# The second half of one feed-forward layer placed between the chunks of the next, normalisations on ScalarE, look-up bits on VectorE

## The reference, cut to what matters

```python
x = x + _L0_xattn_ref(_layernorm(x), ctx_1024, ...)   # 16 heads of 128
x = x + _L0_ffn_ref(_layernorm(x), ...)               # input, weights and hidden in blocks of 32, quantised
x = x + _L1_xattn_ref(_layernorm(x), ctx_1024, ...)   # weights depend on the context alone, applied to norm(x)
x = x + _L1_ffn_ref(_layernorm(x), ...)               # silu(gate) * up, hidden 1024
x = x + _L2_xattn_ref(_layernorm(x), ctx_1024, ...)   # 16 heads of 16, two key groups, q and k normalised
x = x + _L2_ffn_ref(_layernorm(x), ...)               # weights are lut[index], 16 values, hidden 688
x = x + _L3_xattn_ref(ctx_1024, _layernorm(x), ...)   # a state space scan over the context, 16 states
x = x + _L3_ffn_ref(_layernorm(x), ...)               # Hadamard transforms, hidden 1024
```

## Time and profile before

| what | value |
|---|---|
| median of 3 runs (lowest, highest) | 1029.34 us (1029.27, 1031.43) |
| the profiled execution, its span | 1028.96 us, 1027.4 us |
| mean granted TensorE clock, as a share of 2.4 GHz | 0.922 |
| busy: TensorE, VectorE, ScalarE, GpSimd | 867.6, 708.8, 535.8, 448.0 us |
| the chain that ended last, by engine | TensorE 30%, VectorE 14%, ScalarE 4%, GpSimd 1% |

### The profile page before, as it was taken

The page is one execution under the profiler, slowest core; times in us unless marked ns, Lnnn a source line. Parts: engine busy times, 40 slices in busy tenths (PEclk is TensorE's granted clock), DMA queues, the critical chain, the costliest instruction groups (busy, mean ns, idle before and its releaser), DMA issues.

```text
span 1027.4 us, 13071 instructions
## 1 busy us (share of the span) xinstructions
PE 867.6 (84%) x4348; PEld 615.1 (60%) x4352; DVE 708.8 (69%) x1367; ACT 535.8 (52%) x991; POOL 448.0 (44%) x274
## 2 busy tenths in 40 slices
PE   5795899999999999645579986858688799999998
PEld 3354777777877777513354643728577685545646
DVE  4247689999899998778848566765989863353311
ACT  2486687787778778733313442535678472112120
POOL 1211678777778886556810002007458540600000
PEclk8898899999999999866879998958699899999999
DMA  4003000100000100000520000000000001100000
GB/s 126 16 5 133 16 17 16 31 15 15 15 15 15 31 3 6 1 0 1 198 83 0 1 1 1 1 0 1 2 1 2 1 1 48 83 0 1 12 9 21
DMA packets 12924, 24.25 MB, mean 24 GB/s; under 512 B 4280, under 2 KB 8656, under 8 KB 11728
## 3 DMA queue, kind: packets, MB, share of 16 engines
q1 hardware_dynamic: 12448, 20.53, 6.2%
q10 hardware_dynamic: 432, 3.15, 0.8%
HBM read 22.63 MB, written 1.05 MB: 23 GB/s over the span
## 4 chain that ended last, share of the span: by engine, by line
PE 30%; DVE 14%; issue 4%; ACT 4%; POOL 1%; ACTq 0%; DVEq 0%
PE PS L2131 12%; PE PS L2180 6%; PE PS L2234 3%; DVE mxf L1574 2%; DVE regD L1612 1%; PE PS L2035 1%; PE PS L1674 1%; DVE regB L1612 1%; PE PS L2011 1%; PE PS L2198 1%; PE PS L2049 1%; PE PS L2218 1%; PE PS L2219 1%; DVE xn L1051 1%; PE PS L2083 1%
## 5 line engine op out<-in xcount | busy, mean ns | idle before, releaser
L487 POOL TENSOR_TENSOR X<-X,xn 128x512 f32<-128x512 f32 x62 | 103.4, 1668 | 69.1 <-ACT xn L712 68.6
L454 POOL TENSOR_SCALAR veps<-mv 128x4 f32<-128x4 f32 x16 | 3.6, 228 | 265.9 <-DVE mv L1042 265.8
L1141 DVE TENSOR_TENSOR_SCAN regB<-regB 128x1024 f32<-128x1024 f32 x32 | 85.5, 2671 | 0.2
L1122 DVE TENSOR_SCALAR_CACHE_REDUCE regA<-PS,nrq 128x256 bf16<-128x256 f32 x128 | 56.0, 475 | 38.2 <-PE PS L1749 36.3
L731 ACT ACTIVATE regA<-PS,nb,rq 128x256 f32<-128x256 f32 x128 | 72.1, 576 | 11.7 <-DVE regA L1122 10.9
L2234 PE MATMUL PS<-regA 128*128 128x128 f32 x512 | 74.8, 293 | 3.4 <-ACT regA L994 3.3
L480 POOL TENSOR_TENSOR y<-y,regB 128x1024 f32<-128x1024 f32 x32 | 75.7, 2364 | 3.5 <-DVE regB L1152 3.4
L1771 PE MATMUL PS<-regA 128*128 128x256 f32 x256 | 67.0, 384 | 7.3 <-DVE qss L1109 7.2
L2234 PEld LDWEIGHTS PS<-regA 128*128 128x128 f32 x512 | 68.2, 206 | 7.1 <-ACT regA L994 6.1
L1749 PE MATMUL PS<-regA 128*128 128x256 f32 x256 | 67.1, 385 | 0.0
L1780 PE MATMUL PS<-regA 128*128 128x256 f32 x256 | 66.5, 383 | 0.0
(11 more groups left out here) (276 smaller groups left out, 2162.6 us busy)
## 6 DMA issues: line engine op xcount, KB each, us to landing
regA<-in_W SPq DMA_DIRECT2D x16, 384.0 KB, 3.0
regB<-in_wg SPq DMA_DIRECT2D x2, 1024.0 KB, 6.5
regB<-in_wu SPq DMA_DIRECT2D x2, 1024.0 KB, 8.5
X<-in_x SPq DMA_DIRECT2D x1, 1024.0 KB, 8.2
regC<-in_wg ACTq DMA_DIRECT2D x1, 1024.0 KB, 5.8
regC<-in_wu ACTq DMA_DIRECT2D x1, 1024.0 KB, 8.0
regC<-in_wd ACTq DMA_DIRECT2D x1, 1024.0 KB, 10.0
regB<-in_wd SPq DMA_DIRECT2D x1, 1024.0 KB, 9.9
```

Of the source, the lines that this page charges most:

```text
L487: pool.tensor_tensor(xt, xt, part, ALU.add).then_inc(x0_add, 1)
L1122: ins = dve.tensor_scalar(spill[:, i, q, :], bank(S_BANK + i)[:, q * S:(q + 1) * S], nrq[par][:, t:t + 1], None, ALU.mult, ALU.min, accum_ ...
L1141: dve.tensor_tensor_scan(v(hs), v(dA), v(dBu), 0.0, ALU.mult, ALU.add).then_inc(scan_done, 1)
```

## The change

1. *Order.* Layer 0's feed-forward stops after four tiles for the first half's norm, the first half of attention 1 and the second half's; tile 4 and 5's gate and up follow, and tiles 6 and 7, all the second half's transposes and down products, and attention 1's second half are placed between the chunks of layer 1's feed-forward, first half. Attention 1 goes by batches of two tiles. Layer 2's keys begin after chunk 5 of the first half, and its first half's down products and norms lie between them.
2. *Norms 2 to 8.* ScalarE applies them (`ln_apply`), one activation for each tile with rstd as scale and -mean times rstd as bias; GpSimd's `ln_pow` makes that product with two more operations. TensorE transposes by tile. Norms 0, 1 and 9 to 15 stay on VectorE.
3. *Scan.* The last state's decay goes into a buffer of its own (over `u3`), so that ScalarE needn't wait for the state before. Its scans stand behind tile 3; one broadcast of the state before uses another PSUM bank. SP waits for the last scan, not for the last sum, before it loads layer 1's weights.
4. *Look-up.* VectorE makes the three masks and bit 0 by bitwise ands on the integers; ScalarE reads bit 0 as an integer. GpSimd's conversion, comparisons and subtractions go.

```diff
+        ACT_LN = range(2, 9)
 def ln_pow(n):                                          # GpSimd
     pool.wait_ge(ln_mv, n + 1)
-    link(pool.tensor_scalar(veps[:, :], mv[:, :, 1], LN_EPS, None, ALU.add))
-    pool.tensor_tensor(rstd[:, :], veps[:, :], neghalf[:, 0:TPH], ALU.pow).then_inc(ln_rstd, 1)
+    if n >= 3:
+        pool.wait_ge(*xn_ready(n - 1))
+    ready = pool.tensor_scalar(veps[:, :], mv[:, :, 1], LN_EPS, None, ALU.add)
+    if n in ACT_LN:
+        ready = pool.tensor_scalar(nmean[:, :], mv[:, :, 0], -1.0, None, ALU.mult)
+    link(ready)
+    power = pool.tensor_tensor(rstd[:, :], veps[:, :], neghalf[:, 0:TPH], ALU.pow)
+    if n in ACT_LN:
+        link(power)
+        pool.tensor_tensor(nmr[:, :], nmean[:, :], rstd[:, :], ALU.mult).then_inc(ln_rstd, 1)
...
+def ln_apply(n):                                        # ScalarE
+    act.wait_ge(ln_rstd, n + 1)
+    act.wait_ge(*xn_read(n - 1))
+    for t in range(TPH):
+        act.activation(xn[:, t, :], X[:, t0 + t, :], ACT.Identity, scale=rstd[:, t:t + 1],
+                       bias=nmr[:, t:t + 1]).then_inc(xn_tile, 1)
...
-            sp.wait_ge(wt_out, 6)
-            sp.wait_ge(y_done, 2 * NST + 1)
+            sp.wait_ge(scan_done, 2 * NST + 1)
             for tile, name in ((wf_g, "wg1"), (wf_u, "wu1"), (wf_d, "wd1")):
                 sp.dma_start(tile, a[name]).then_inc(ld_f1, 16)
+            sp.wait_ge(wt_out, 6)
...
 # VectorE, layer 0's feed-forward, after the new order
+            x_scales(0)
+            x_units(0)
+            round_values(rows(xv), rows(x8))
+            layer_norm_stats(3)
             state_scan(NST - 2, 1)
...
+            ffn0_gated(3)
+            ffn0_round(2)
+            ffn0_add(0)
+            layer_norm_tiles(4, (0,))
+            state_in(NST - 1, 0)
...
+            layer_norm_mean(4)
+            state_scan(NST - 1, 0)
+            state_scan(NST - 1, 1)
+            attend1_add(0)
+            layer_norm_tiles(5, (0, 1))
+            attend1_add(1)
...
+            state_out(NST - 1, 0)
+            ffn0_gated(4)
+            state_out(NST - 1, 1)
+            ffn0_round(4)
+            ffn0_gated(5)
+            gate(0, 0, 0)
+            ffn0_round(5)
+            gate(0, 0, 1)
+            ffn0_gated(6)
...
+            ffn0_add(7)
+            layer_norm_stats(6)
+            dve.wait_ge(y_done, 2 * NST + 1)
+            keys_step(0)
+            gate(0, 0, 6)
+            keys_step(1)
+            gate(0, 0, 7)
+            keys_step(2)
+            ffn_add(0, 0, 0)
+            attend1_add(2)
+            attend1_add(3)
+            layer_norm_stats(7)
...
 # TensorE, layer 1's feed-forward, first half
+            for c in range(FC):
+                if c < 2:
+                    pe.wait_ge(h0_done, 11 + c)
...
+                gate_up(0, 0, c, wf_g, wf_u, half[0])
+                if c == 1:
+                    ffn0_gate_up(6)
+                    hidden_transpose(4)
+                elif c == 2:
+                    ffn0_down(4)
+                    hidden_transpose(5)
+                    ffn0_gate_up(7)
+                elif c in (3, 4):
+                    ffn0_down(c + 2)
+                    hidden_transpose(c + 3)
+                elif c == 5:
+                    ffn0_down(7)
+                    pe.wait_ge(ld_2, 16 * 13)
+                    keys_values(0)
+            pe.wait_ge(kv2_out, 3)
+            ln_transpose(6)
+            down(0, 0, 0, wf_d)
...
+            attend1(2)
+            pe.wait_ge(df_add, 1)
+            attend1(3)
+            pe.wait_ge(x1_add, 3)
+            down(0, 0, 1, wf_d)
+            keys_values(1)
...
 def lut_step(i, step):                                  # VectorE
     A = w2[:, i * LP:(i + 1) * LP]
+    if step == 0:
+        for m, bit in zip(lut_m[i % 2], (2, 4, 8)):
+            dve.tensor_scalar(m.bitcast(I32), A.bitcast(I32), bit, None, ALU.bitwise_and).then_inc(lut_mask, 1)
+        dve.tensor_scalar(lut_b0[i % 2].bitcast(I32), A.bitcast(I32), 1, None, ALU.bitwise_and).then_inc(lut_bits, 1)
```

More of the change, by code:

```diff
@@ L196, in build @@
         invx, scx = [inv8[1], sb("mx_ix", [P, BLK])], [sc8[2], sb("mx_sx", [P, BLK])]
-        QX = [0, 2]
-        QH = [1] + [tt + 2 for tt in range(1, NT)]
+        QX = [0, 5]
+        QH = [1, 2, 3, 4, 6, 7, 8, 9]
         wq1, wk1 = tA(P), tA(P)
@@ L719, in decay @@
                     act.wait_ge(scan_done, 1)
+                elif isinstance(n, int) and n == NST - 1:
+                    act.wait_ge(zero_set, 1)
+                    act.activation(dA_last[:, c, :, 1:], dt3[:, c, :, 1:], ACT.Exp,
+                                   scale=A3[:, c, n:n + 1]).then_inc(dA_done, 1)
+                    return
                 else:
@@ L2106, in scan_transpose, with gate_up, down, ffn @@
                     last.then_inc(z_tr, 1)
-            def ffn(f, wg, wu, wd, nch):
-                hid = INTER2 if f == 1 else FF
+            def gate_up(f, hf, c, wg, wu, src):
+                i = CB[2 * f + hf] + c
+                rows = min(P, (INTER2 if f == 1 else FF) - c * P)
+                for w, to in ((wg, 2 + i % 2), (wu, 4 + i % 2)):
+                    for k in range(KD):
+                        last = pe.matmul(bank(to)[0:rows, :], w[:, k, c * P:c * P + rows], src[:, k, :],
+                                         start=k == 0, stop=k == KD - 1)
+                last.then_inc(guf_mm, 1)
+            def down(f, hf, t, wd):
+                td = TPH * (2 * f + hf) + t
+                nch = FCH[f]
+                for c in range(nch):
+                    rows = min(P, (INTER2 if f == 1 else FF) - c * P)
+                    if t == 0:
+                        pe.wait_ge(gated, CB[2 * f + hf] + c + 1)
+                    last = pe.matmul(bank(6 + td % 2)[:, 0:DIM], hT[0:rows, c, t * P:(t + 1) * P], wd[0:rows, c, :],
+                                     start=c == 0, stop=c == nch - 1)
+                last.then_inc(df_mm, 1)
+            def ffn(f, wg, wu, wd):
                 for hf in range(2):
@@ L2175, in ffn @@
                             ln_transpose(13)
-                        for c in range(nch):
-                            rows = min(P, hid - c * P)
-                            if t == 0:
-                                pe.wait_ge(gated, CB[m] + c + 1)
-                            last = pe.matmul(bank(6 + td % 2)[:, 0:DIM], hT[0:rows, c, t * P:(t + 1) * P], wd[0:rows, c, :],
-                                             start=c == 0, stop=c == nch - 1)
-                        last.then_inc(df_mm, 1)
@@ L2183, in ffn @@
-                        if f == 0 and hf and 1 <= t <= 2:
-                            pe.wait_ge(q2_out, 1)
-                            keys_step(4 * B + t)
-            ln_transpose(5)
-            pe.wait_ge(ld_f1, 48)
-            pe.wait_ge(ld_2, 16 * 13)
-            ffn(0, wf_g, wf_u, wf_d, FC)
+                        down(f, hf, t, wd)
+            half = [xnT[:, :, hf * HALF:(hf + 1) * HALF] for hf in range(2)]
+            pe.wait_ge(ld_f1, 48)
+            pe.wait_ge(ssm_use, 4 * NST + 1)
@@ new lines, in _ @@
+            ln_transpose(7)
+            pe.wait_ge(df_add, 2)
+            down(0, 0, 3, wf_d)
+            pe.wait_ge(xnT_done, TRANSPOSED.index(7) + 1)
+            keys_step(6)
+            for c in range(FC):
+                if c in (1, 5):
+                    if c == 1:
+                        pe.wait_ge(df_add, TPH)
+                    keys_values((7 + c) // 4)
+                pe.wait_ge(gated, FC + c - 1)
+                gate_up(0, 1, c, wf_g, wf_u, half[1])
+                keys_step(7 + c)
+                if c == 4:
+                    pe.wait_ge(stk_out, 8)
+                    ln_transpose(8)
@@ L2191, in scores @@
+            pe.wait_ge(stk_out, 12)
+            queries(0)
+            pe.wait_ge(kv2_out, 12)
+            for t in range(TPH):
+                pe.wait_ge(df_add, TPH + t - 1)
+                down(0, 1, t, wf_d)
+                if 1 <= t <= 2:
+                    pe.wait_ge(q2_out, 1)
+                    keys_step(4 * B + t)
             def scores(b, h):
```

565 lines of the change are left out of this document (319 added, 246 removed).

## The result

The changed kernel takes 1021.62 us (median of 4 runs, 1021.07 to 1023.47) against 1029.39 (1029.27 to 1031.43, 4 runs) beside it; the ratio is 0.9915, interval 0.9903 to 0.9926. The forecast was 1003, 989 to 1018: the direction is right, but where 26 us were forecast, 7.8 came.

A forecast was written before the change was run, and what follows sets the result against it. A serial VectorE stage (quantising, with GpSimd) before a serial TensorE stage was taken to bound the kernel; 25.7 us from reordering plus 0.4 from look-up bits, 26 off 1028.96, gave 1003 us, range 989 to 1018.

The forecast's parts named there:

- first chunk: Start of the second layer's feed-forward on TensorE: forecast at 499 in place of 529.7, a gain of 30.7 us.
- merged stretch: From the first chunk to the end of that layer's last down product: 141 us against 136.0, bounds 126 and 151.
- look-up stage: From that last down product to the next layer's first chunk, third attention included: 185.9 us, 0.4 gained.
- Start of the tiles: First layer's feed-forward: normalisation on ScalarE and an earlier first block maximum start the first tile's matmuls near 437, 3.8 us earlier.
- Tiles 0 to 3: First layer's feed-forward: VectorE pays some 4.3 us per tile; fourth gating at 461, its addition at 471, scans 472 to 477.
- First half of attention 1 moved up: Second attention's first half before the first chunk: GpSimd's power ends at 478, banks free at 496, 3 us allowed for collisions.
- rival C: More is gained: TensorE's clock stays at 2.4 GHz, no collisions, bits hide; 4 + 4 + 5 us more, 990; chance 0.12.
- Look-up bits: Third attention: bits on VectorE cost 13.8 us, conditional copies lose 12.0; net 0.4 gained, bounds 12 gained and 14 lost.
- rival D: Slower: VectorE's bits open gaps before TensorE in the third attention and its clock falls; 1039; chance 0.05.
- A: Rival: the merged stretch becomes bound by VectorE, 151 us in place of 141; 1013; chance 0.18 together with E.
- E: Rival: normalisation on ScalarE gives nothing, as its queue stands at it; 3.8 and 4 us go, 1011; 0.18 with A.
- B: Rival: the look-up bits cost all they add, 14 us lost rather than 0.4 gained; 1017; chance 0.10.

The follow-up runs named there:

- experiment 6: Changed kernel with one added wait: VectorE starts the last two scans only once GpSimd has made the fourth layer norm's factors; 1013.54 us, ratio 0.983.
- experiment 7: Changed kernel with 18 extra, unused TensorE matmuls in its 4.5 us of idle time before the fourth layer norm's transposes; 1018.71 us, ratio 0.9887.
- experiment 9: Changed kernel with experiment 6's wait, shift weights made by ScalarE, and ScalarE's eighth layer norm copies put ahead of its key casts; 998.07 us, ratio 0.9691.
- experiment 5: Changed kernel with layer norms 2 to 8 applied by VectorE again, new order and look-up bits kept; 1020.22 us, ratio 0.9891.
- experiment 3: Changed kernel with experiment 6's wait and the look-up bits back on GpSimd; 1014.94 us, ratio 0.984.

## Why the prediction was wrong, step by step

The span came out 18.2 us above the forecast's 1001.4. The first chunk was 10.8 us late (509.8, not 499), the merged stretch 13.4 too long (154.4, not 141), and the look-up stage 6.0 shorter than forecast. Two steps failed: the path from tile 0 to the first chunk, above all the first half of attention 1, where I priced GpSimd's wait for the scans but not the idle TensorE and the low clock behind it; and the length of the second half's chunks in the merged stretch, 55.8 us where I had 46.9. That the direction was right is in large part luck: of the 19.9 us won, 18.4 were given back, and 6.4 of the 7.8 us of gain come from a stage for which I had 0.4.

*What bounds the kernel.* Right in kind: moving the feed-forward up shortened the serial VectorE stage, and what is won ahead of the first chunk arrives at the end (7.0 for 6.8 us in experiment 6, 3.0 for 3.2 in experiment 7). *Start of the tiles:* 439.1, not 437. GpSimd made the factors when it had before (from 426.3), so the 2.1 us arose in the block. About 1 of them is my arithmetic: 0.6 added and 0.55 and 0.6 saved make 433.5 for the end of the quantising, not 432.5. Besides, ScalarE's four activations took 2.07 us and not 1.8, and one 128x32 scaling took 1.13 in place of 0.18, beside a GpSimd addition.

*Tiles 0 to 3.* The fourth gating started at 463.1 (forecast: 461), as late as the first tile had been. From there the additions slipped: the fourth one started at 477.8, not 471. My cost per tile left out that the second half's quantising itself collides (its product takes 2.93 us, where the first half's took 1.23; two roundings take 2.89 us, one alone 0.69), and that the additions wait for TensorE, which waits for GpSimd's products. This is one part of the failed path to the first chunk: at the fourth layer norm's mean 7.1 us are lost (479.1, not 472).

*First half of attention 1 moved up.* Here the other half fails. That GpSimd waits out the scans was in the forecast and happened, 484.9 being 1.4 us behind the scans' end; the Trainium skill's rule that the port pair is held for a whole instruction (SBUF — State Buffer, Who interferes with whom) agrees with 2.11 against 0.23 us. What I didn't see is the consequence: the wait puts TensorE to idle and then to the low level, and with one engine's result feeding the next, every lengthened matmul is on the chain. From the fourth layer norm's mean to the fifth's I gave 16 us (472 to 488); it took 20.1 (479.1 to 499.2), and 10.6 more to the first chunk, for which I gave 8 and 3 of allowance. Experiments 6 and 7 show it: the two groups of attention matmuls alone take 3.5 us less at the full level, and with the one wait added, mean to mean takes 12.5 us. I had counted the low level as a gain of rival C if it went away, never as a cost of the new order. Of 10.8 us of lateness at the first chunk, one wait that lets GpSimd go first takes 6.8 off.

*Weights.* Right: they were issued behind the scans, and no wait for them is seen in any version.

*The merged stretch*, 141 with 151 as its upper bound, was 154.4. Its pieces by my own milestones, counted from the first chunk (496 in the forecast, 509.8 here):

| | forecast | measured |
|---|---|---|
| end of chunk 5 | 30 | 33.2 |
| end of chunk 7 | 41 | 43.6 |
| last down product of the first half | 68.6 | 73.5 |
| last chunk of the second half | 115.5 | 129.3 |
| last down product | 139.6 | 154.4 |

The largest miss, 8.9 us, is in the second half's chunks, for which I allowed 46.9 us. The kernel before takes 51.8 for the same chunks (from 593.2 to 645.0), so 5 us of the miss are a step that I should have checked against the trace. The other 4 are what the wait for ScalarE's copies grew by (4.16 us, 1.76 before) and the low level behind it (the keys' products take 4.51 us, 2.81 before); in experiment 9 the same moves win 4.7 us back. TensorE was busy 130.4 us where I had 126: 10.5 of moved work and not 9, on 118.5 where I had cut out 117, and some 1.4 left over, which I put down to the lower clock. My bound of 151 (its terms, 136.0, 3.6 and 12.5, make 152) assumed that only VectorE's queue can lengthen the stretch; ScalarE's order did too. "The shift weights still collide" was right, with the same 8.2 us; that a wait of this size costs 2.4 more behind it I had not seen (the kernel before pays 1.8 of that too, so it lengthened the stretch little).

*Look-up bits.* The prices were right: 0.432 us an instruction against 0.43, and the copies fell to 42.56 us in 56 from 54.06, 11.5 less against 12.0 (window of that line alone in the changed kernel, columns as in the earlier trace rows):

```profile
684.00:844.00 160.00, 42.56 (x56) 0.89 0.00 1
```

The sum was wrong. Against this order's GpSimd bits the move gains 1.1 us (forecast 0.4), but the kernel before paid 5.2 us more, most of it at two clock drops, and these went too. I had a loss of clock in this stage only as rival D, as a cost of bits on VectorE. Drops late in the stage were met only with bits on GpSimd, in two of three programs, and two of the three drops came behind a copy that a GpSimd instruction had held up.

*The rivals.* A (a stretch of 151, 1013) came nearest by the stretch's length, but for another reason: VectorE was busy 100.8 of 154.6 us there, no more than I gave it. E's outcome came, that normalisation on ScalarE gives nothing in sum (experiment 5), but not by its reason: it is VectorE's order, scans beside GpSimd's factors, that takes back ahead of the first chunk what the merged stretch gains. B, C and D did not happen. Of the marks that I named, the idle time of TensorE under 25 us was kept (24.2, in a longer stretch), GpSimd is silent in the look-up stage (2.5 us), the addition still takes 7.5 us; the first chunk, the last down product and the stage's unchanged length fell outside, two late and one short.

## What to carry to other kernels

A wait that leaves TensorE idle for some us is paid twice: once as the wait, once in slower matmuls behind it, and the second part can be as large (experiment 7: 3 us behind 4.5 idle; experiment 9: 2.4 behind 2.4). So in a forecast give every serial exchange between engines its price at the low level, unless the rows show TensorE busy ahead of it, and look for a small operation that stands beside a long one of VectorE or GpSimd: letting the long one wait (one line here) was worth about as much as the whole change. Where a stage is only moved, take its length from its own rows and add to it; a length built up from parts was 5 us short. And split a gain by stage before calling a forecast's direction right: here one stage gave most of it, for a reason that wasn't in the forecast.

## What the runs showed of the hardware

- A GpSimd operation of 128x4 takes 0.23 us alone and 2.11 beside VectorE's scan, a VectorE addition of 128x512 takes 0.68 alone and 7.51 beside GpSimd's instruction of 7.12. ScalarE makes the same weights in 16 activations of 96x256 in 6.50 us, and that VectorE addition takes 0.68.
- Two instructions that start 0.01 us apart can go either way: GpSimd's subtraction and VectorE's conditional copy of 128x536 took 1.91 and 0.76 us in one program, 1.32 and 1.93 in another. In the second case TensorE waited 2.38 us in place of 1.21 and its clock fell; the stage took 3.4 us more than 181.
- In the same stage TensorE fell to the low level in one program and not in another, equally busy in the 4 us ahead (2.01 and 2.03 us of work, then a granted clock of 0.57 and 1.00). Time lost at one late drop: 1.7 us and 2.4 us in the kernel before, 2.3 in experiment 3. The longer low stretches earlier in that stage cost nothing at its end (granted 0.86 and 0.89 on average, 180 us both).
